# Local attention on one core: the 64 block sums placed in the unused half of the key window, with GpSimd laying mixed rows of values

## The reference, cut to what matters

```python
LOCAL_RADIUS, TOKENS_PER_BLOCK, NEG = 127, 16, -1e9
bl = 128; nb = 8; G = 64
q = einsum('bld,dhk->blhk', x, Wq) / sqrt(64); k = ...Wk; v = ...Wv
g = einsum('bld,lg->bgd', x, one_hot)          # 64 sums of 16 tokens each
side_k = einsum('bgd,dhk->bghk', g, Wk); side_v = ...Wv
kb, vb = three neighbouring blocks of 128 keys / values for each block of 128 queries
logits = q . [kb, side_k]                       # 384 + 64 columns
rel = k_idx - bl - q_idx
valid = (abs(rel) <= LOCAL_RADIUS) & (k_pos >= 0) & (k_pos < L)
logits += where(valid, 0, NEG)                  # the 64 sums are never masked
unnorm = exp(x - m); denom = unnorm.sum + exp(-m)   # softmax with an extra logit 0
y = probs . [vb, side_v]; out = einsum('blhk,hkd->bld', y, Wo)
```

## Time and profile before

| | us |
|---|---|
| median of 3 runs | 1963.37 |
| lowest, highest | 1960.29, 1978.29 |
| span of the profiled execution (first to last instruction) | 1966.6 |
| part of the span in phase f's loop (first scores to the first instruction of the next phase) | 1318.1 to 1862.0 |

### The profile page before, as it was taken

The page is one execution under the profiler, slowest core; times in us unless marked ns, Lnnn a source line. Parts: engine busy times, 40 slices in busy tenths (PEclk is TensorE's granted clock), DMA queues, the critical chain, the costliest instruction groups (busy, mean ns, idle before and its releaser), DMA issues.

```text
span 1966.6 us, 38046 instructions
## 1 busy us (share of the span) xinstructions
PE 1847.9 (94%) x15770; PEld 1344.2 (68%) x15770; DVE 1106.2 (56%) x2301; ACT 943.0 (48%) x1689; POOL 465.6 (24%) x512
## 2 busy tenths in 40 slices
PE   6999899959999958999999999989999999999997
PEld 3467775745566725677777777757777777787776
DVE  4585750053332247788888798825555544455544
ACT  2213122103333226788888888835555544444522
POOL 1362210013320252121121112013232322233212
PEclk9979799979999979999999999999999999999999
DMA  4000032112444457611012101000000000010001
GB/s 136 0 1 2 1 90 71 44 34 74 132 140 136 139 175 176 92 32 39 21 40 93 39 21 39 2 22 1 2 1 2 1 1 1 1 28 1 2 0 43
DMA packets 89309, 92.22 MB, mean 47 GB/s; under 512 B 34914, under 2 KB 74786, under 8 KB 88994
## 3 DMA queue, kind: packets, MB, share of 16 engines
q1 hardware_dynamic: 82882, 78.01, 14.1%
q0 software_dynamic: 3456, 9.44, 1.8%
q10 hardware_dynamic: 2800, 2.34, 0.4%
HBM read 67.23 MB, written 23.07 MB: 46 GB/s over the span
## 4 chain that ended last, share of the span: by engine, by line
PE 87%; DVE 5%; ACT 2%; DMA 2%; issue 2%; POOL 1%; another core or an unknown queue 0%; SPq 0%; POOLq 0%; DVEq 0%
PE PS L1646 13%; PE PS L1096 8%; PE PS L1105 8%; PE PS L1660 7%; PE PS L1971 6%; PE PS L2016 6%; PE PS L2032 6%; PE PS L1637 6%; PE PS L2006 5%; PE PS L1976 3%; PE PS L549 3%; PE PS L2039 1%; PE PS L2071 1%; PE PS L493 1%; PE PS L2351 1%
## 5 line engine op out<-in xcount | busy, mean ns | idle before, releaser
L1819 DVE CUSTOM_DVE_ANT_0 arena<-PS,arena 128x1024 f32<-128x1024 f32 x256 | 312.0, 1219 | 61.5 <-PE PS L1637 57.6
L1740 ACT ACTIVATE arena<-arena 128x1024 f32<-128x1024 f32 x256 | 296.7, 1159 | 9.6 <-DVE arena L1819 9.2
L1646 PE MATMUL PS<-arena 128*128 128x128 f32 x2048 | 279.5, 279 | 5.4 <-issue 4.8
L1646 PEld LDWEIGHTS PS<-arena 128*128 128x128 f32 x2048 | 230.1, 142 | 65.6 <-issue 32.3
L2219 POOL TENSOR_SCALAR arena<-arena 128x448 f32<-128x448 f32 (+1 forms) x256 | 153.4, 616 | 393.6 <-DVE arena L2147 392.6
L2118 ACT ACTIVATE arena<-arena 128x449 f32<-128x449 f32 (+1 forms) x256 | 161.4, 632 | 141.2 <-DVE arena L2156 141.2
L1736 ACT COPY arena<-PS 128x512 f32<-128x512 f32 x298 | 170.0, 585 | 65.8 <-PE PS L1646 63.3
L1096 PE MATMUL PS<-arena 128*128 128x512 f32 x384 | 170.7, 602 | 6.6 <-ACT arena L1202 6.6
L2156 DVE CUSTOM_DVE_ANT_0 arena<-PS,arena 128x448 f32<-128x448 f32 (+1 forms) x256 | 136.7, 588 | 59.9 <-PE PS L2007 58.8
L1105 PE MATMUL PS<-arena 128*128 128x256 f32 x768 | 168.8, 379 | 0.0
L1105 PEld LDWEIGHTS PS<-arena 128*128 128x128 f32 x768 | 144.7, 189 | 22.2 <-issue 1.4
(11 more groups left out here) (294 smaller groups left out, 2671.0 us busy)
## 6 DMA issues: line engine op xcount, KB each, us to landing
arena<-in_L_ffn_W SPq DMA_DIRECT2D x16, 1024.0 KB, 7.4
arena<-prior SPq DMA_DIRECT2D x16, 512.0 KB, 4.6
parts<-arena SPq DMA_DIRECT2D x24, 256.0 KB, 5.6
arena<-parts SPq DMA_DIRECT2D x96, 64.0 KB, 2.8
arena<-parts SPq DMA_DIRECT2D x48, 128.0 KB, 7.3
prior<-arena SPq DMA_DIRECT2D x4, 1024.0 KB
ye<-arena SPq DMA_DIRECT2D x7, 512.0 KB, 3.0
ya<-arena SPq DMA_DIRECT2D x7, 512.0 KB, 4.8
```

Source lines behind the costliest of these rows:

```text
L1646: h = e.transpose(PS[:, i, P * j:P * j + P], Sb[z % 3][:, 512 * g + P * j:512 * g + P * j + P], ident)
L1740: e.activation(Sb[z % 3], Sb[z % 3], ACT.Exp, bias=mr[:, z % 4:z % 4 + 1], scale=-1.0).then_inc(s_exp, 1)
L1819: e.tensor_tensor_reduce(Sb[z % 3], ps, Ab[m % 2], 1.0, 3e38, ALU.add, ALU.min, mr[:, z % 4:z % 4 + 1]).then_inc(s_ttr, 1)
```

## The change

Scores of an inner tile get 384 columns in lieu of 448. The block sums' scores are put where half a tile has no keys: for the queries 0 to 63 into columns 320 to 383, for the queries 64 to 127 into columns 0 to 63. For that each head's scores are made by four matmuls in lieu of two, each with 64 stationary columns (half of the queries). Edge tiles get the same four-way form with 256 + 64 columns. All tiles have three transpositions for each head. Since the 128 rows of a turned tile now mix sums and values (for half of the queries only), `values` of an inner tile has five matmuls for each head in lieu of four, one of 128 moving columns and four of 64, and takes two of its stationary tiles from VM, which GpSimd lays: `whole(z)` copies the values of the block before and the block sums, `upper(z)` writes rows 0 to 63 of the one with the sums and of the other with the values of the block behind. Edge tiles take the sums from a VM tile with a cleared lower half. `side` writes the sums' values to both halves of the partitions, so that sv needs no clearing.

```diff
-    K.f_band, K.f_space, K.f_load = arena.up(768), flat(K6[0]).bitcast(F32)[:, 2 * S:8 * S], None
+    K.f_band, K.f_space, K.f_load = arena.up(896), flat(K6[0]).bitcast(F32)[:, 2 * S:8 * S], None
...
-    Sb = [arena.up(449) for _ in range(3)]
+    Sb = [arena.up(385) for _ in range(3)]
     Se = [arena.up(321) for _ in range(2)]
-    Pb = [arena.up(512) for _ in range(8)]
-    Pt = [arena.up(512) for _ in range(4)]
+    Pb = [arena.up(385) for _ in range(8)]
+    Pt = [arena.up(384) for _ in range(4)]
+    VM = [arena.up(2 * P).rearrange("p (a c) -> p a c", a=2) for _ in range(4)]
...
+    def n_whole(z):
+        t = z % 8
+        return 14 * (z // 8) + (14 if t == 7 else 1 + 2 * t)
...
 # side, values of the sums
-                    h = e.matmul(PS[0:64, i, :], gT[:, s[1], k, :], Wv5[:, k, 512 * s[2]:512 * s[2] + 512], start=k == 0, stop=k == 1)
+                    for r in range(2):
+                        h = e.matmul(PS[64 * r:64 * r + 64, i, :], gT[:, s[1], k, :], Wv5[:, k, 512 * s[2]:512 * s[2] + 512], start=k == 0, stop=k == 1)
...
 # scores
-                q_ = q5[r][rows, P * t:P * t + P]
-                e.matmul(PS[:, x % 4, 0:nk], q_, k5[r][rows, P * k0:P * k1], start=True, stop=True)
-                e.matmul(PS[:, x % 4, nk:nk + 64], q_, sk[rows, u % 8, u // 8, :], start=True, stop=True).then_inc(s_sc, 1)
+                side_ = sk[rows, u % 8, u // 8, :]
+                q_ = [q5[r][rows, P * t + 64 * g:P * t + 64 * g + 64] for g in range(2)]
+                out = [PS[64 * g:64 * g + 64, x % 4, :] for g in range(2)]
+                if inner(z):
+                    e.matmul(out[0][:, 0:320], q_[0], k5[r][rows, k0:k0 + 320], start=True, stop=True)
+                    e.matmul(out[1][:, 64:384], q_[1], k5[r][rows, k0 + 64:k0 + 384], start=True, stop=True)
+                    e.matmul(out[0][:, 320:384], q_[0], side_, start=True, stop=True)
+                    e.matmul(out[1][:, 0:64], q_[1], side_, start=True, stop=True).then_inc(s_sc, 1)
+                else:
+                    e.matmul(out[0][:, 0:256], q_[0], k5[r][rows, k0:k0 + 256], start=True, stop=True)
+                    e.matmul(out[1][:, 0:256], q_[1], k5[r][rows, k0:k0 + 256], start=True, stop=True)
+                    e.matmul(out[0][:, 256:320], q_[0], side_, start=True, stop=True)
+                    e.matmul(out[1][:, 256:320], q_[1], side_, start=True, stop=True).then_inc(s_sc, 1)
...
 # turn
-                for j in range(nj):
+                for j in range(3):
...
 # values
+            w.wait_ge(s_vm, n_vm(z))
+            if inner(z):
+                work = [(natural(k0 + 1), 1, 0, P), (natural(k0), 0, 0, 64), (vm[:, 0], 0, 64, P), (vm[:, 1], 2, 0, 64), (natural(k0 + 2), 2, 64, P)]
+            else:
+                work = [(natural(k0), 0, 0, P), (natural(k0 + 1), 1, 0, P), (vm[:, 0], 2, 0, P)]
+            for m, (wt, j, lo, hi) in enumerate(work):
                 for d in range(2):
-                    c = slice(64 * d, 64 * d + 64)
-                    wt = v5[r][:, P * (k0 + j):P * (k0 + j) + P][:, c] if j < nj - 1 else sv[u // 8][:, u % 8, c]
-                    h = e.matmul(PS[c, YB, P * (t % 4):P * (t % 4) + P], wt, Pt[(2 * z + d) % 4][:, P * j:P * j + P], start=j == 0, stop=j == nj - 1)
+                    c, o = slice(64 * d, 64 * d + 64), P * (z % 4)
+                    h = e.matmul(PS[c, YB, o + lo:o + hi], wt[:, c], Pt[(2 * z + d) % 4][:, P * j + lo:P * j + hi], start=m == 0, stop=m == len(work) - 1)
...
 # side_out
-            w.wait_ge(s_zero, N_ZERO)
-            h = e.copy(sv[s[1]][0:64, ...], PS[0:64, i, :])
+            h = e.copy(sv[s[1]][:, ...], PS[:, i, :])
...
 # pool
+        def whole(z):
+            u, t, vm = z // 8, z % 8, VM[z % 4]
+            w.wait_ge(s_val, z - 3)
+            if inner(z):
+                w.wait_ge(*first.emptied(("sv", 1, 1)))
+                w.wait_ge(*of(u).emptied((u, 4)))
+                w.wait_ge(*of(u).emptied((u, 5)))
+                e.tensor_copy(vm[:, 0], v5[u % 2][:, P * (t - 1):P * t]).then_inc(s_vw, 1)
+                e.tensor_copy(vm[:, 1], sv[u // 8][:, u % 8, :]).then_inc(s_vw, 1)
+            else:
+                e.memset(vm[:, 0], 0.0).then_inc(s_vw, 1)
+
+        def upper(z):
+            u, t, vm = z // 8, z % 8, VM[z % 4]
+            w.wait_ge(*first.emptied(("sv", 1, 1)))
+            w.wait_ge(s_vw, n_whole(z))
+            e.tensor_copy(vm[0:64, 0], sv[u // 8][0:64, u % 8, :]).then_inc(s_vm, 1)
+            if inner(z):
+                e.tensor_copy(vm[0:64, 1], v5[u % 2][0:64, P * (t + 1):P * (t + 2)]).then_inc(s_vm, 1)
+
         K.e_done(w)
-        for z in sv:
-            e.memset(z, 0.0).then_inc(s_zero, 1)
...
                 e.tensor_scalar(Pb[x % 8][:, 0:wd], Pb[x % 8][:, 0:wd], sm[:, g:g + 1], 1.0, ALU.mult, ALU.mult).then_inc(s_norm, 1)
+            whole(z)
+            if z:
+                upper(z - 1)
+        upper(NZ - 1)
```

More of the change, by code:

```diff
@@ L1905, in phase_f, with inner, first_key, width @@
     s_tc = [K.sem("f_probs_act"), K.sem("f_probs_dve")]
-    def geom(z):
+    s_vw, s_vm = K.sem("f_mixed_whole"), K.sem("f_mixed")
+    def inner(z):
+        return 0 < z % 8 < 7
+    def first_key(z):
+        return max(z % 8 - 1, 0)
+    def width(z):
+        return 3 * P if inner(z) else 2 * P + 64
+    def n_whole(z):
         t = z % 8
-        k0, k1 = max(t - 1, 0), min(t + 2, 8)
-        return k0, k1, P * (k1 - k0)
+        return 14 * (z // 8) + (14 if t == 7 else 1 + 2 * t)
+    n_vm = n_whole
     def chunk_by(c):
@@ L2019, in values @@
         def values(z):
[L2020 to L2023, removed]
+            u, n = z // 8, z // 4
+            v, k0, vm = v5[u % 2], first_key(z), VM[z % 4]
             for d in range(2):
@@ L2026, in values, with natural @@
             w.wait_ge(*of(u).emptied((u, 5)))
+            w.wait_ge(s_vm, n_vm(z))
             w.wait_ge(s_y, n)
-            for j in range(nj):
+            def natural(k):
+                return v[:, P * k:P * k + P]
+            if inner(z):
[3 more added lines that the diff above has]
+            for m, (wt, j, lo, hi) in enumerate(work):
                 for d in range(2):
-                    c = slice(64 * d, 64 * d + 64)
-                    wt = v5[r][:, P * (k0 + j):P * (k0 + j) + P][:, c] if j < nj - 1 else sv[u // 8][:, u % 8, c]
-                    h = e.matmul(PS[c, YB, P * (t % 4):P * (t % 4) + P], wt, Pt[(2 * z + d) % 4][:, P * j:P * j + P], start=j == 0, stop=j == nj - 1)
+                    c, o = slice(64 * d, 64 * d + 64), P * (z % 4)
+                    h = e.matmul(PS[c, YB, o + lo:o + hi], wt[:, c], Pt[(2 * z + d) % 4][:, P * j + lo:P * j + hi], start=m == 0, stop=m == len(work) - 1)
             h.then_inc(s_val, 1)
@@ L2098, in side_out @@
         else:
-            w.wait_ge(s_zero, N_ZERO)
-            h = e.copy(sv[s[1]][0:64, 4 * s[2]:4 * s[2] + 4, :].rearrange("p f n -> p (f n)"), PS[0:64, i, :])
+            h = e.copy(sv[s[1]][:, 4 * s[2]:4 * s[2] + 4, :].rearrange("p f n -> p (f n)"), PS[:, i, :])
         h.then_inc(first.into(s), 1)
@@ L2120, in turn @@
         def turn(z):
-            n = geom(z)[2] + P
             w.wait_ge(s_tf, 2 * z + 1)
             w.wait_ge(s_val, z - 1)
-            e.copy(Pt[2 * z % 4][:, 0:n], PS[:, 4, 0:n]).then_inc(s_tc[0], 1)
+            e.copy(Pt[2 * z % 4], PS[:, 4, 0:384]).then_inc(s_tc[0], 1)
         for c in (0, 1, 4, 5):
@@ L2594, in layouts @@
     nxt = np.where(i[None, :] < i[:, None], np.float32(0), -NEG)
-    a["k_band"] = np.concatenate([prev, z, nxt, z[:, :64], prev, z, z[:, :64]], axis=1).astype(np.float32)
+    inner = np.concatenate([prev, z, nxt], axis=1)
+    inner[:64, 320:], inner[64:, :64] = 0, 0
+    a["k_band"] = np.concatenate([inner, prev, z, z[:, :64], nxt, z[:, :64]], axis=1).astype(np.float32)
     a["k_iota"] = np.broadcast_to(np.concatenate([np.arange(P) + 1, np.arange(32) - 32]).astype(np.float32), (P, 160))
```

22 lines of the change are left out of this document (10 added, 12 removed).

## The result

The changed kernel takes **1906.19 us** (median of 4 runs, 1904.59 to 1912.89); the kernel before took 1970.83 beside it (median of 4). The ratio is 0.9689, 95% interval 0.9640 to 0.9739. The prediction said 1913 within 1904 to 1942 and faster by over 1% with 0.85: the time lies in the range, near its lower end, and the forecast's ratio, 1913 / 1963.37 = 0.9744, lies just above the interval. Ratios and intervals here compare only runs that count as fast, and so need not be the quotients of the medians given, in which three slower runs of the kernel before still count (1994.10, 2001.76 and 4699.27 us).

The account below looks back on a forecast made before the run. TensorE's stream was taken as the bound; turn 16.2, values 17.3 and scores 17.0 sum to 50.5 us off the 1966.6 us span, giving 1916.1, and 1913 us as the runs' median. Range 1904 to 1942 us.

Parts of the forecast that it names:

- The bound: Phase f's loop: TensorE busy nearly throughout, so time off its stream is time off the whole, unless a wait grows.
- Turn: Transpositions of an inner tile: two fewer save 0.218 us, except where bank 7 waits hide them; 16.2 us in all.
- turn of an inner tile 0.65 for six: Expected sign in the new trace: an inner tile's six transpositions take 0.65 us on TensorE.
- Values: Values matmuls of inner tiles: new form of 64-column steps at 0.059 us gains 0.18 us a tile, 17.3 us.
- Scores: Scores matmuls by four quarters side by side: fewer columns and a smaller fixed part, 17.0 us.
- This 0.054 is paid twice in a pair today: Scores: extra step behind a 128-column weight load, at the pair's start and where the second tile's load follows the sums.
- The prediction's bound: Upper limit for the scores' gain: all four fixed loads vanish, 20 us at best.
- GpSimd: Its added scaling and copies, at 0.3 us a copy, stay covered in the loop and cost nothing.
- Rival (a): Scores: a head's two halves run in turn; 1991 to 1998 us, slower by 1.4 to 1.8%; chance 0.09.
- Rival (b): GpSimd's copies bound the loop from 0.75 us each; at 0.85 the time is about 1953 us; chance 0.07.
- Rival (c): TensorE's other waits, such as bank 7, eat a third of the gain: 1921 to 1940 us; chance 0.12.
- The rest: VectorE and ScalarE off the path give nothing; side's extra matmuls cost 0 side by side, 6.9 us in a row.

Follow-up runs that it names:

- second kernel of halves: Kernel before with scores by halves of 64 stationary columns, each half of an inner tile also omitting its 64 masked columns: 1945.12 us, ratio 0.9891.
- first kernel of halves: Kernel before with each scores matmul of 128 stationary columns split into two of 64, same moving columns: 1962.24 us, ratio 0.9988.
- the version with the early chunk: Changed kernel with the first of two users of bank 7 moved between scores and values: 1919.57 us, ratio 0.9689; run again 1910.43 us, 0.9695.

## Why the prediction was right

- **The bound.** "A nanosecond off TensorE's stream is a nanosecond off the time" held: the three parts fell by 57.7 us by the distances between starts, and the loop by 57.3.
- **Turn, 16.2 us forecast, 15.9 measured.** 0.218 for an inner tile came out (0.929 to 0.711), and so did the places without gain: 0.946 to 0.948 in the second turn of the pair with query chunks, 0.840 to 0.841 in the one ahead of it in the unit, 0.87 to 0.84 beside a projection. The sign "turn of an inner tile 0.65 for six" left out the 0.06 at the change of form that the sum had counted; it is 0.71. The fourth transposition put back cost 15.5.
- **Values, 17.3 forecast, 18.8 measured.** Two inner tiles fell by 0.393, from 1.913 to 1.520, an inner beside an edge tile by 0.196, from 1.692 to 1.496: 0.196 a tile in both, instead of 0.18. Eight steps of 64 columns cost 0.057 each by that, where L566 gave 0.059; the price was nearly right.
- **Scores, 17.0 forecast, 23.0 measured: this term was mis-sized.** The columns were right: 10.2 us, shown by the step from the first to the second kernel of halves. The mistake is in "This 0.054 is paid twice in a pair today (at its start, and where the second tile's load follows the sums)". The first kernel of halves takes 0.201 and 0.200 out of the pairs with no column less, in four places: the two that the prediction names, and two more, the second tile's own first records (0.05) and the way from its sums to the values (0.04). 64 x 0.20 = 12.8 us instead of 7 accounts for the 6 us. The prediction's bound has all four: "at best all four fixed loads vanish, 20 us". That sum is wrong; two more loads of 0.054 in each of 64 pairs on top of 17.0 are 24 us, and the 23.0 measured lie under that. That it is the load which shortens each place is inferred: the loads became 0.053 us shorter and the columns stayed the same, but the number of matmuls doubled with them.
- **GpSimd, 0 forecast, 0 measured** at 0.29 us a copy (0.3 forecast). The price at which it would matter was named as 0.75 from a sum over the unit. Doubled, it cost 2.1 us, all at the loop's end. Tripled, at 0.74 and so just under that threshold, it cost 21.0. The sum over a unit says where GpSimd becomes the bound, but the step took "costs nothing" for all that lies below it; the cost begins earlier, at the end of the loop and in single pairs.
- **Rival (a)**, halves of one row group take turns, fell with the quarters that start within 0.04 us and with the reordered quarters at 0.02. `side` shows it too: its 512-column matmuls for the sums' values take 7.08 us before (L1991, 16 records) and 7.09 after (L2007, 32 records, the second half in the same rows), so this term was 0 as forecast. The Trainium skill's rule in TensorE: Matmul & The Clock Gate, section Part 3: Packing small matmuls, is that weight loads overlap running matmuls only where the row group differs, and that matmuls start and end strictly in program order. The trace disagrees: in `side` loads and matmuls of a second half in the same rows add 0.01 us, and with the quarters reordered a matmul started 0.58 us ahead of one issued before it. The Trainium skill's TensorEngine Tiling, section Tiling Modes, lets different tiles load weights and multiply in parallel, with four tiles of 64 x 64. The trace agrees: the four start within 0.04 us and run 0.48 us each.
- **Rival (b)**, GpSimd as the bound, is seen only with four times the copies; with three times it is late without being the bound. **Rival (c)**, new waits, came in a small part: the waits at bank 7 doubled to 8.7 us, mostly where the forecast had written the gain off; chunks and projections grew by 0.5 us together.
- **The rest.** Chunks 164.1 to 164.3. The stretch behind the loop lost 0.8 us, the phases ahead of it took 2.5 more. Neither needs the change for a cause: two profiles of the changed kernel start the loop at 1320.6 and 1325.4 us and have 103.8 and 104.7 behind it, and two of the version with the early chunk start it at 1334.3 and 1311.4. The granted clock differs there as well: from 200 to 400 us it is 0.95 in the profile of before and 0.88 in that of after, while both have 1.00 in the seven units of the loop.

## What to carry to other kernels

When an engine is busy for all of a stretch, price an edit by the distances between starts of the same forms elsewhere in the trace, and take the places where a wait hides the work out of the sum one by one: turn came out within 2% that way, values within 9%. Halving the stationary tile saved time even where every half passed all columns (0.20 us in a pair of tiles); count every load of a short stream, not those at its edges. Where the whole time varies by more than the gain, compare the stretch that was changed, or runs with the same granted clock. An engine that has room over a whole unit can still be late in its densest part and at the loop's end, and a gap on TensorE can cost the clock of the work behind it as well: one of 3.91 us did each time, those of up to 1.9 us in the loop's body never did.

## What was not expected of the hardware

- Idle times of 3.91 us were each followed by work at half speed, at a granted clock of 0.50 where it was read, durations 1.7 to 1.9 times as long (turn 0.71 to 1.33, chunk 1.72 to 2.90). Behind idle times of 1.6 us (copies three times) and 1.9 us (four times) the turn kept its 0.71. Behind 2.93 us it kept it twice (at 1348.78 and 1795.37 us) and took 1.29 once (at 1834.09), so the length of the gap alone doesn't decide.
- The order in which four quarters are issued made 0.013 us in a pair.
- The same chunk costs 1.72 us ahead of a turn and 1.92 ahead of scores or values, whose tiles are smaller than 128 x 128.
- Weight loads and matmuls of two column halves in the same rows cost no more than one half: 7.08 and 7.09 us in `side`.
- The phases ahead of the loop, all but the same in all these kernels, end between 1307.6 and 1334.3 us: more than any of the smaller effects tried here.
